# Turning the normalised rows of five pairs by DMA instead of TensorE, and grouping the half-width products, in a one-core attention and feed-forward kernel

## The chip, the core and the metric

The kernel runs on one core of one Trainium2 chip. The metric is the device time of one launch in microseconds; the median of three runs before the change is 612.24 us (612.08 to 613.53).

## The reference

`x` is 16 sequences of 64 rows of 1024; `ctx_4096` is 16 matrices of 1024 x 1024, all float32. Cut to what is computed:

```python
def fake_quant(x, s, z):
    return (clip(round(x / s + z), 0, 255) - z) * s

x = x + matmul(fake_quant(layernorm(x)), fake_quant(ctx_4096))      # one matrix per sequence
h = layernorm(x)
q, k, v = split(h @ qkv_w + qkv_b, 3)                               # 32 heads of 32
q, k = rope(q), rope(k)
p = softmax(q @ k.T / sqrt(32) + causal mask)
x = x + (p @ v) @ out_w + out_b
h = layernorm(x)
x = x + h @ W.T + bias + sum_e coeffs[e] * scales[e] * (h @ A[e].T) @ Bf[e].T
```

## The kernel before, in words

The rows of two sequences form a pair of 128 rows; there are eight pairs, 0 to 7. For each pair the kernel does the quantised cross product with its two context matrices, then attention; the feed-forward stage follows for all pairs. Every large product is made of float16 parts: operands are split into a high and a low float16 part, and `dense` (L1347) makes three products for each of eight slices of 128: high by high, high by low, low by high. A tile is 128 rows by 512 columns in one PSUM bank, 24 products.

The five engines have programs of their own, joined by semaphores, and the order on each is written out by hand. TensorE's order sets the plan: `next_pair(i, ahead)` (L1700) makes the six projection tiles of pair `i` with `qkv(i, j, between)` (L1447), where `between` is a table {slice: [steps]} of what else is issued behind which slice. Among these steps:

- `codes` turns the quantised rows of pair `i + 1` (eight float16 transposes, L1436), and ScalarE evacuates them in `a_high` (L385); `codes_turned` waits for that. `t(...)`, which is `cross` (L1406), multiplies them with the context codes. From pair 3 on ("tiled") one product has half the width of the array (128 by 64) and two run side by side; `shifted`, `cross_shift` (L1422), adds a correction from the sums of all codes. The products come in four groups of eight, behind slices of tiles 2, 2, 3 and 5, and the shift in a fifth group.
- `qk_turn`, `scores`, `p_turn` and `values` are the attention of pair `i`. `project` (L1538) is the output projection in four parts of twelve products. After the second, `x_turn(i + 1)` turns the normalised rows of the next pair: eight float32 transposes (`turn`, L1344) into the PSUM banks T.

The turned rows are evacuated by ScalarE as the high float16 part (`x_high`, L380) and by VectorE as the low one (`x_low`, L933). TensorE starts pair `i + 1` when `s_xl` says that both are there. VectorE makes the rows in `norm2` (L924): statistics, a chain of small operations for the reciprocal root, then `lnt = (x - mean) * factor`. Before that it needs `tiled_evac` (L955), which needs the shift products, which need `sums_as_f16` (L950), which needs GpSimd's sums of all 16 code chunks (`add_codes`, L800).

The context comes in 16 chunks of 512 KB for each pair. SP loads them (`load_chunk`, L650; order in `next_set`, L723) into three slots in turn: the two halves of `raw`, and `lnt`, which is also where the normalised rows lie until they are turned. Chunk `c` uses slot `c % 3`; chunk 2, the first one in `lnt`, waits for the row turn. ScalarE quantises a chunk into one of eight places of a ring `code` (`quantise`, L357); a place is free again when TensorE and GpSimd have used it. ScalarE's order is in `next_pair` (L493): two chunks of pair `i + 2` at the end of pair `i`, then chunks 2 to 5 of the next, `a_high`, and the rest between evacuations and exponentials. ScalarE also issues the load of the rows of pair `i + 2` (`rows_after_next`, L400).

In the last stage rows are turned by DMA already: `rows_high` (L621) writes float16 rows and issues a transposing DMA from ScalarE's queue, VectorE's `rows_low` (L1272) makes the low rows, and `rows_low_turned` (L632) turns them.

Of the kernel before, what the change touches and what calls it, by code (L numbers as in the profile page):

```python
# [55 lines left out]
def build(nc, x, ctx_in, consts, qkv_w, out_w, bias_rows, out_bias, ffn_wt, ffn_bias, lora_a, lora_b, lora_w, out):  # L56
# [6 lines left out]
    with es:  # L63
# [51 lines left out]
        uses = [len(range(n, CHUNKS, 3)) for n in range(3)]  # L115
# [10 lines left out]
        d16 = pr[:, 0, :].bitcast(F16)  # L126
        acc_words = acc[:, :].bitcast(I32).rearrange("p (b n) -> p b n", b=2)
# [62 lines left out]
        s_xl = sem("s_xl")  # L190
        s_u8 = sem("s_u8")
# [144 lines left out]
        def _(act):  # L336
# [20 lines left out]
            def quantise(i, c):  # L357
# [3 lines left out]
                else:  # L361
                    n = c % 3
                    src = slots[n].rearrange("p (a n) -> p a n", a=2)
                    if isinstance(i, int) and i == 1:
                        src = chunk1_stage(c)
                        act.wait_ge(s_ctx0[c], 32)
                    else:
                        act.wait_ge(s_slot[n], 16 * (uses[n] * (i - 2) + c // 3 + 1))
# [124 lines left out]
            def next_pair(i, more, late=False):  # L493
# [7 lines left out]
                w(25)  # L501
                q(2)
                if not late:
                    q(3, 4, 5)
                a_high(i + 1, 0)
                a_high(i + 1, 1)
                if late:
                    q(3, 4)
# [3 lines left out]
                qk_evac(i, 0)  # L512
                if not late:
                    q(6)
                q(7, 8)
                w(28)
                qk_evac(i, 1)
                q(9)
                w(29)
                q(10)  # L520
                if late:
                    q(11)
                exponent(i, 0)
                if not isinstance(i, int) or i < PAIRS - 2:
                    rows_after_next(i)
                q(12 if late else 11)
                exponent(i, 1)
                qk_evac(i, 2)
                if not late:
                    q(12)  # L530
                q(13)
                p_evac(i, 0)
                if late:
# [7 lines left out]
                else:  # L541
                    q(14)
# [14 lines left out]
                x_high(i + 1, 0)  # L557
                x_high(i + 1, 1)
                if late:
                    value_bias()  # L560

# [47 lines left out]
            with act.Fori(2, PAIRS - 2) as i:  # L609
# [39 lines left out]
        def _(sp):  # L649
            def load_chunk(i, c):  # L650
# [7 lines left out]
                n = c % 3  # L658
# [1225 lines left out]
```

## Time and profile before

| | |
|---|---|
| Median of 3 runs | 612.24 us |
| The profiled execution's own time | 612.36 us |
| Its span | 610.3 us |
| Granted clock, mean | 1.0 of full |
| TensorE products (PE) busy | 588.4 us, 96% |
| VectorE (DVE) busy | 467.0 us, 77% |
| ScalarE (ACT) busy | 292.8 us, 48% |
| GpSimd (POOL) busy | 125.4 us, 21% |
| Chain that ended last, by engine | PE 79%, DVE 11%, SPq 4%, DMA 3% |

PE, DVE, ACT and POOL are TensorE, VectorE, ScalarE and GpSimd; PEld is TensorE's weight load, SP issues DMAs. A row of a timeline gives start, length, engine, line, operation, output <- input, shapes and count; in brackets stands how long the engine was idle before it, and who ended that. Product durations overlap in the pipeline, so the distance of two starts is what a product costs in a stream. "DMA to landing" is the time from the issue of a transfer to its completion.

### The profile page before, as it was taken

To read this page: it belongs to the slowest core of one execution; us is meant where nothing else is said; L and a number is where in the kernel's file an instruction comes from. 1 tells how busy PE (TensorE), PEld (TensorE's weight loads), DVE (VectorE), ACT (ScalarE), POOL (GpSimd) and SP (SyncE) were. 2 spreads that over 40 slices of the span, in tenths; PEclk is the share of its full clock that TensorE was granted. 3 is DMA by queue.
4 is the path that set the end of the run, shared out by engine and by line. 5 is a ranking of instruction groups with operands and counts; after the bars stand their busy time and mean duration, and the time that the engine had idled before them with its cause. 6 is when DMAs were issued, how large, how long until landed. Compare 5 with 4: busy or idle time off the path is not lost.

```text
span 610.3 us, 12961 instructions
## 1 busy us (share of the span) xinstructions
PE 588.4 (96%) x4921; PEld 295.1 (48%) x4921; DVE 467.0 (77%) x931; ACT 292.8 (48%) x359; POOL 125.4 (21%) x173
## 2 busy tenths in 40 slices
PE   3889999999999999999999999999999999999998
PEld 1464455455545445544455445545445554444445
DVE  6999998778777866786677868678864789987751
ACT  5977695865456435634553464546331242210100
POOL 4000010000165234613541354345100000000000
PEclk9999999999999999999999999999999999999999
DMA  8999996861356255507531673265222025477541
GB/s 319 387 387 361 393 361 227 287 225 71 132 188 233 71 201 205 180 35 275 203 141 50 224 237 107 114 208 194 103 92 81 1 89 223 122 147 154 144 107 53
DMA packets 53698, 111.83 MB, mean 183 GB/s; under 512 B 18586, under 2 KB 18970, under 8 KB 53664
## 3 DMA queue, kind: packets, MB, share of 16 engines
q1 hardware_dynamic: 37744, 104.35, 49.4%
q10 hardware_dynamic: 15648, 6.48, 4.6%
q0 software_dynamic: 272, 0.55, 0.2%
q8 instruction: 21, 0.34, 0.2%
q14 instruction: 13, 0.11, 0.1%
HBM read 99.30 MB, written 8.39 MB: 176 GB/s over the span
## 4 chain that ended last, share of the span: by engine, by line
PE 79%; DVE 11%; SPq 4%; DMA 3%; issue 2%; ACT 1%; ACTq 0%; DVEq 0%
PE dense L1353 15%; PE dense L1355 15%; PE dense L1354 15%; PE turn L1344 5%; PE dense L1547 4%; PE dense L1549 4%; PE dense L1548 4%; DVE wq L941 4%; PE cross L1417 3%; PE score L1508 3%; PE dense L1563 2%; SPq L656 2%; DMA wq<-in_qkv_w 2%; PE cross L1402 2%; PE score L1534 2%
## 5 line engine op out<-in xcount | busy, mean ns | idle before, releaser
L1353 PE MATMUL dense<-wq,xn_h 128*128 128x512 f16 x400 | 152.2, 380 | 1.3 <-DMA xn_l<-spare 0.9
L1354 PE MATMUL dense<-wq,xn_h 128*128 128x512 f16 x400 | 151.6, 379 | 0.0
L1355 PE MATMUL dense<-wq,xn_l 128*128 128x512 f16 x400 | 151.6, 379 | 0.0
L811 POOL TENSOR_TENSOR acc<-code,acc 128x256 int32<-128x256 int32 x140 | 104.0, 773 | 114.1 <-ACT code L378 114.1
L378 ACT ACTIVATE code<-raw,cst,qc 128x1024 uint8<-128x1024 f32 x72 | 87.3, 1237 | 13.4 <-DMA raw<-in_ctx 12.9
L1353 PEld LDWEIGHTS dense<-wq,xn_h 128*128 128x128 f16 x400 | 39.0, 97 | 50.6 <-issue 14.0
L1355 PEld LDWEIGHTS dense<-wq,xn_l 128*128 128x128 f16 x400 | 39.1, 98 | 47.3
L1354 PEld LDWEIGHTS dense<-wq,xn_h 128*128 128x128 f16 x400 | 39.2, 98 | 34.9
L378 ACT ACTIVATE code<-lnt,cst,qc 128x1024 uint8<-128x1024 f32 x32 | 39.6, 1237 | 27.0 <-DMA lnt<-in_ctx 26.5
L998 DVE SCALAR_TENSOR_TENSOR at<-cst,score 128x512 f32<-128x512 f16 x24 | 16.4, 684 | 40.1 <-PE score L1508 40.1
L1547 PE MATMUL dense<-wo,rope 128*128 128x512 f16 x112 | 42.5, 379 | 0.8 <-DVE rope L1028 0.8
L1549 PE MATMUL dense<-wo,rope 128*128 128x512 f16 x112 | 42.4, 379 | 0.0
L1548 PE MATMUL dense<-wo,rope 128*128 128x512 f16 x112 | 42.4, 379 | 0.0
L407 ACT ACTIVATE at<-at 128x512 f32<-128x512 f32 x32 | 20.0, 628 | 37.5 <-DVE at L1004 37.4
L394 ACT ACTIVATE at<-turn 128x512 f32<-128x512 f32 x32 | 19.0, 593 | 37.2 <-PE turn L1344 24.0
L811 POOL TENSOR_TENSOR acc<-code,lw 128x256 int32<-128x256 int32 x20 | 11.6, 613 | 116.4 <-ACT code L378 116.4
L413 ACT ACTIVATE at<-turn 128x512 f32<-128x512 f32 x32 | 19.0, 592 | 32.3 <-PE turn L1344 32.2
L626 ACT ACTIVATE spare<-lnt 128x1024 f16<-128x1024 f32 x7 | 7.4, 1057 | 54.1 <-DVE lnt L1259 54.1
L1402 PE MATMUL cross<-code,q1t 128*128 128x512 f16 x96 | 28.3, 392 | 3.2 <-DVE xa L948 1.5
L984 DVE TENSOR_TENSOR rope<-dense,cst 128x512 f32<-128x512 f32 x32 | 22.0, 689 | 11.2 <-PE dense L1355 8.3
L990 DVE TENSOR_TENSOR rope<-rope 128x512 f32<-128x512 f32 x32 | 24.5, 766 | 1.4
L1035 DVE SCALAR_TENSOR_TENSOR xa<-dense,xa 128x512 f32<-128x512 f32 x16 | 11.0, 690 | 18.1 <-PE dense L1549 18.0
(225 smaller groups left out, 1036.3 us busy)
## 6 DMA issues: line engine op xcount, KB each, us to landing
raw<-in_ctx SPq DMA_DIRECT2D x72, 512.0 KB, 4.4
lnt<-in_ctx SPq DMA_DIRECT2D x32, 512.0 KB, 4.2
wo<-in_ctx SPq DMA_DIRECT2D x16, 512.0 KB, 8.8
wo<-in_qkv_w SPq DMA_DIRECT2D x12, 512.0 KB, 11.7
wq<-in_qkv_w SPq DMA_DIRECT2D x8, 512.0 KB, 11.9
x_scratch<-xa SPq DMA_DIRECT2D x8, 512.0 KB, 3.0
wq<-in_ctx SPq DMA_DIRECT2D x7, 512.0 KB, 11.7
wo<-in_out_w SPq DMA_DIRECT2D x7, 512.0 KB, 6.9
```

Of the source, the lines that this page charges most:

```text
L378: act.activation(low_bytes, src, ACT.Identity, scale=qc[:, 1:2], bias=z2).then_inc(s_u8, 1)
L811: ins = pool.tensor_tensor(sums[:, cols], words[:, cols], acc_from.to_broadcast([P, half]) if c < 2 else sums[:, cols], ALU.add)
L941: dve.scalar_tensor_tensor(lo, staged(j), WSC, hi, ALU.mult, ALU.subtract).then_inc(s_wlo, 1)
L990: dve.tensor_tensor(rope[:, 2 + j % 2, :], rope[:, 0, :], rope[:, 1, :], ALU.add).then_inc(s_qr, 1)
L1344: ins = pe.transpose(bank[:, k * P:(k + 1) * P], src[:, c:c + P], ident)
L1353: pe.matmul(bank[:, :], a_h[:, k, :], w_hi, start=(k == 0 and not started), stop=False)
L1354: pe.matmul(bank[:, :], a_h[:, k, :], w_lo, start=False, stop=False)
L1355: ins = pe.matmul(bank[:, :], a_l[:, k, :], w_hi, start=False, stop=(k == KC - 1 and not last))
L1402: ins = pe.matmul(X[n][:, :], lhs, code[:, c % RING, n * NT:(n + 1) * NT], start=(kc == 0), stop=(kc == KC - 1))
L1547: pe.matmul(D[n][:, :], c_h[:, k, :], wo_h[:, k, cols], start=(k == 0), stop=False)
L1548: pe.matmul(D[n][:, :], c_h[:, k, :], wo_l[:, k, cols], start=False, stop=False)
L1549: ins = pe.matmul(D[n][:, :], c_l[:, k, :], wo_h[:, k, cols], start=False, stop=(k == KC - 1))
```

## The change

1. **Rows by DMA.** For pairs 3 to 7 `x_turn`, `x_high` and `x_low` go. ScalarE computes the high float16 rows straight from `xb` with factor and bias (`rows_turned`) and turns them by a transposing DMA into `xn_h`; VectorE writes the low rows (`x_rows_low`), and ScalarE issues their turn into `xn_l`. The float16 rows lie in `pr`, the tile of the softmax. The first projection tile of such a pair makes its sixteen products with the high rows first, and then waits for the low ones.
2. **Chunks.** The first six chunks alternate between the halves of `raw`; `lnt` is used by chunks 6, 9, 12 and 15. SP loads six chunks of pair `i + 2` ahead, but holds the fifth (and what follows) until the low turn of the pair before has landed. ScalarE quantises four chunks of pair `i + 2` at the end of pair `i`.
3. **Products.** Code products come in two groups of sixteen: behind the last slice of tile 2, and behind slice 1 of tile 5, there with the shift.
4. VectorE casts the code sums before `softmax_in(i, 3)`. The loops of ScalarE and SP over pairs 2 to 5 are written out.

```diff
+        slot_of = [c % 2 if c < 6 else (c - 4) % 3 for c in range(CHUNKS)]
+        x_hl = [pr[:, n, :].bitcast(F16) for n in range(2)]
...
+            def rows_turned(i):
+
+                act.wait_ge(s_xfac, i - TILED + 1)
+                act.activation(x_hl[0], xb[:, :], ACT.Identity, scale=nw[:, 0:1], bias=nw[:, 3:4]).then_inc(s_xrowh, 1)
+                act.wait_ge(s_xrowh, i - TILED + 1)
+                act.wait_ge(s_qkv, 6 * i)
+                act.dma_start_transpose(xn_h[:, :, :], x_hl[0]).then_inc(s_xturnh, 16)
+                act.wait_ge(s_xt, 2 * i + 2)
+                act.dma_start_transpose(xn_l[:, :, :], x_hl[1]).then_inc(s_xturnl, 16)
...
+                    q(4, 5, 6, 7)
+                    a_high(i + 1, 0)
+                    a_high(i + 1, 1)
+                    qk_evac(i, 0)
+                    qk_evac(i, 1)
+                    q(8)
+                    exponent(i, 0)
+                    if not isinstance(i, int) or i < PAIRS - 2:
+                        rows_after_next(i)
+                    q(9, 10)
+                    exponent(i, 1)
+                    q(11)
+                    qk_evac(i, 2)
+                    q(12)
+                    p_evac(i, 0)
+                    q(13)
                     qk_evac(i, 3)
-                    q(15)
+                    q(14, 15)
                     p_evac(i, 1)
                 exponent(i, 2)
+                if more:
+                    quantise(i + 2, 0)
                 exponent(i, 3)
+                if more:
+                    quantise(i + 2, 1)
...
                 if more:
-                    quantise(i + 2, 0)
-                    quantise(i + 2, 1)
+                    quantise(i + 2, 2)
+                    quantise(i + 2, 3)
                 c_high(i, 1)
...
+                else:
+                    rows_turned(i + 1)
...
-                if c == 2:
+                if c < 2:
+                    sp.wait_ge(s_u8, CHUNKS * i + c - (1 if isinstance(i, int) and i == 2 else 2))
+                elif c < 6:
+                    sp.wait_ge(s_u8, CHUNKS * i + c - 1)
+                    if c == 4 and tiled(i):
+                        sp.wait_ge(s_xturnl, 16 * (i - 2))
+                elif c == 6:
                     sp.wait_ge(s_xt, 2 * i)
...
+            def x_rows_low(i):
+                dve.wait_ge(s_xn, i + 1)
+                dve.wait_ge(s_xrowh, i - TILED + 1)
+                dve.tensor_tensor(x_hl[1], lnt[:, :], x_hl[0], ALU.subtract).then_inc(s_xt, 2)
...
+                    for k in range(KC):
+                        for w in (wq_h, wq_l):
+                            pe.matmul(D[0][:, :], xn_h[:, k, :], w[:, k, n * NT:(n + 1) * NT], start=(k == 0 and w is wq_h), stop=False)
+                    pe.wait_ge(s_xturnl, 16 * (i - 1))
+                    for k in range(KC):
+                        pe.matmul(D[0][:, :], xn_l[:, k, :], wq_h[:, k, n * NT:(n + 1) * NT], start=False, stop=False)
...
-                    qkv(i, 2, {1: [at(t, 0, 1)], 3: [at(codes_turned, 1), at(qk_turn, i, 1)], 4: [at(m, 1)], 6: [at(middle_biases, i), at(scores, i, 0)], 7: [at(t, 2, 3)]})
+                    qkv(i, 2, {4: [at(codes_turned, 1), at(qk_turn, i, 1), at(m, 1)], 6: [at(middle_biases, i), at(scores, i, 0)], 7: [at(t, 0, 1, 2, 3)]})
...
-                    qkv(i, 3, {2: [at(m, 2)], 5: [at(t, 4, 5)], 6: [at(turned, i, 1), at(qk_turn, i, 2)]})
+                    qkv(i, 3, {2: [at(m, 2)], 6: [at(turned, i, 1), at(qk_turn, i, 2)]})
...
-                    qkv(i, 5, {0: [at(t, 6, 7)], 1: [at(m, 4)], 2: [at(m, 5)], 3: [at(values_due, i, 0)], 4: [at(values, i, 0)],
-                               6: [at(shifted), at(evacuated, i, 0), at(p_turn, i, 2)], 7: [at(p_turn, i, 3)]})
+                    qkv(i, 5, {1: [at(t, 4, 5, 6, 7), at(shifted), at(m, 4)], 2: [at(m, 5)], 3: [at(values_due, i, 0)], 4: [at(values, i, 0)],
+                               6: [at(evacuated, i, 0), at(p_turn, i, 2)], 7: [at(p_turn, i, 3)]})
...
-                if ahead:
+                if late:
                     x_turn(i + 1)
```

## Rows read from the trace of the kernel before

**Rows 1.** the page: busy us and its share; granted clock in 40 slices
```profile
PE 588.4 (96%) x4921; PEld 295.1 (48%) x4921; DVE 467.0 (77%) x931; ACT 292.8 (48%) x359; POOL 125.4 (21%) x173
...
PEclk9999999999999999999999999999999999999999
```

**Rows 2.** windows: one pair, busy us of each engine, clock, DMA
```profile
332.00:389.00 57.00, 56.77 (x541) 28.18 (x539) 42.53 (x88) 29.26 (x36) 22.98 (x32) 1.00 0.49 166
```

**Rows 3.** the chain of waits: start us, us, what, at the row turns
```profile
331.36 0.87 PE turn L1344 x8
...
388.60 0.87 PE turn L1344 x8
```

**Rows 4.** the timeline of TensorE in pair 5: tile starts
```profile
337.25 0.38 PE L1353 MATMUL dense<-wq,xn_h 128*128 128x512 f16 x1
...
347.84 0.60 PE L1344 MATMUL turn<-cst,rope 128*128 128x128 f32 x4
```

**Rows 5.** the timeline of TensorE around the row turn
```profile
330.98 0.38 PE L1549 MATMUL dense<-wo,rope 128*128 128x512 f16 x1
331.20 1.04 PE L1344 MATMUL turn<-cst,lnt 128*128 128x128 f32 x8
332.07 0.38 PE L1547 MATMUL dense<-wo,rope 128*128 128x512 f16 x1
```

**Rows 6.** row turns of L1344: duration ns min/median/max, first and last start
```profile
L1344 PE MATMUL turn<-cst,lnt x72: 272/273/328, 37.1 to 512.7; 128*128 128x128 f32 x72
```

**Rows 7.** the timeline of TensorE around one group of half-width products
```profile
350.00 0.38 PE L1355 MATMUL dense<-wq,xn_l 128*128 128x512 f16 x1
350.31 1.05 PE L1417 MATMUL cross<-code,q1t 128*64 128x512 f16 x8
351.30 0.39 PE L1353 MATMUL dense<-wq,xn_h 128*128 128x512 f16 x1
```

**Rows 8.** VectorE's timeline from the second scores to the pair's end
```profile
371.64 0.69 DVE L998 SCALAR_TENSOR_TENSOR at<-cst,score 128x512 f32<-128x512 f16 x1 [2.16 <-PE score L1508]
...
381.48 0.75 DVE L1028 SCALAR_TENSOR_TENSOR rope<-score,rope 128x256 f16<-128x256 f32 x2
...
382.74 0.68 DVE L846 BATCH_NORM_STATS2 st<-xb 128x6 f32<-128x512 f32 x1
...
386.53 0.81 DVE L931 TENSOR_SCALAR lnt<-xb,mv,nw 128x1024 f32<-128x1024 f32 x1
```

**Rows 9.** the timeline of TensorE at the start of the output projection
```profile
382.37 0.38 PE L1547 MATMUL dense<-wo,rope 128*128 128x512 f16 x1 [0.16 <-DVE rope L1028]
```

**Rows 10.** the timeline of the last stage, a row turn by DMA
```profile
544.68 1.06 ACT L626 ACTIVATE spare<-lnt 128x1024 f16<-128x1024 f32 x1 [7.39 <-DVE lnt L1259]
...
545.76 1.31 ACTq L630 DMA_TRANSPOSE q1t<-spare  x1
545.77 1.23 DVE L1276 TENSOR_TENSOR spare<-lnt,spare 128x1024 f16<-128x1024 f32 x1 [0.52 <-ACT spare L626]
```

**Rows 11.** the instructions on xn_l: its transposing DMAs
```profile
DMA to landing us min/median/max: 3.7/6.1/7.0
```

**Rows 12.** DMA issues: count, median us to landing; the turns into q1t
```profile
q1t<-spare ACTq DMA_TRANSPOSE x8, 3.5
```

**Rows 13.** the timeline of ScalarE at a pair's start
```profile
335.91 1.24 ACT L378 ACTIVATE code<-lnt,cst,qc 128x1024 uint8<-128x1024 f32 x1 [2.99 <-DMA lnt<-in_ctx]
338.44 2.44 ACT L378 ACTIVATE code<-raw,cst,qc 128x1024 uint8<-128x1024 f32 x2 [1.28 <-DMA raw<-in_ctx]
...
345.87 1.08 ACT L387 ACTIVATE q1t<-turn 128x512 f16<-128x512 f32 x2 [0.54 <-PE turn L1436]
```

**Rows 14.** instructions of L679, SP's chunk loads from 325 to 400
```profile
DMA to landing us min/median/max: 3.1/4.7/7.3
```

**Rows 15.** the timeline of GpSimd, sums of the last four chunks
```profile
366.38 6.43 POOL L811 TENSOR_TENSOR acc<-code,acc 128x256 int32<-128x256 int32 x8 [4.08 <-ACT code L378]
```

**Rows 16.** the instructions of L403, loads of a later pair's rows
```profile
DMA to landing us min/median/max: 4.0/6.8/7.3
```

More of the change, by code:

```diff
@@ L114, in build @@
         slots = [raw[:, 0, :], raw[:, 1, :], lnt[:, :]]
-        uses = [len(range(n, CHUNKS, 3)) for n in range(3)]
+        slot_of = [c % 2 if c < 6 else (c - 4) % 3 for c in range(CHUNKS)]
+        uses = [slot_of.count(n) for n in range(3)]
         value_stage = [at_stage[:, 1, :, :], at_stage[:, 0, :, :], at_stage[:, 2, :, :], spare[:, :].rearrange("p (a n) -> p a n", a=2)] + o_stage[0:4]
@@ L190, in build @@
         s_xl = sem("s_xl")
+        s_xfac = sem("s_xfac")
+        s_xrowh = sem("s_xrowh")
+        s_xturnh = sem("s_xturnh")
+        s_xturnl = sem("s_xturnl")
         s_u8 = sem("s_u8")
@@ L500, in w @@
                         weight_hi(j)
[L501 to L506, printed above, removed]
                 if late:
+                    w(25)
+                    q(2)
+                    a_high(i + 1, 0)
+                    a_high(i + 1, 1)
                     q(3, 4)
@@ L511, in next_pair @@
                     w(27)
[L512 to L524, printed above, removed]
+                    qk_evac(i, 0)
+                    q(7, 8)
+                    w(28)
+                    qk_evac(i, 1)
+                    q(9)
+                    w(29)
+                    q(10, 11)
+                    exponent(i, 0)
                     rows_after_next(i)
[L526 to L529, printed above, removed]
                     q(12)
-                q(13)
-                p_evac(i, 0)
-                if late:
+                    exponent(i, 1)
+                    qk_evac(i, 2)
+                    q(13)
+                    p_evac(i, 0)
                     p_evac(i, 1)
@@ L608, in _ @@
             next_pair(1, True, True)
-            with act.Fori(2, PAIRS - 2) as i:
+            for i in range(2, PAIRS - 2):
                 next_pair(i, True)
@@ L657, in load_chunk @@
                     return
-                n = c % 3
+                n = slot_of[c]
                 if isinstance(i, int) and i == 1:
@@ L1126, in next_pair @@
                 softmax_in(i, 2)
+                if not late:
+                    sums_as_f16(i + 1)
                 softmax_in(i, 3)
@@ L1144, in next_pair @@
                 c_low(i, 1)
-                x_low(i + 1, 0)
-                x_low(i + 1, 1)
+                if late:
+                    x_low(i + 1, 0)
+                    x_low(i + 1, 1)
+                else:
+                    x_rows_low(i + 1)
                 out_evac(i, 0)
@@ L1726, in codes_turned @@
                         pe.wait_ge(s_ah, 2 * i + 3 + e)
-                pe.wait_ge(s_xl, 2 * i + 2)
+                if isinstance(i, int) and i == 1:
+                    pe.wait_ge(s_xl, 2 * i + 2)
+                else:
+                    pe.wait_ge(s_pte, 4 * i)
+                    pe.wait_ge(s_xturnh, 16 * (i - 1))
                 if isinstance(i, int) and i == 1:
```

49 lines of the change are left out of this document (31 added, 18 removed).

## The prediction

> **What bounds the kernel now.** First the page's busy shares: TensorE is busy for 588.4 of 610.3 us and its granted clock stands at the upper level, 2.4 GHz, in every slice [rows 1]. Then the windows by pair: one steady pair has 56.77 us of TensorE in 57.00, with VectorE at 42.53 and ScalarE at 29.26 [rows 2]. The chain of waits shows the same point of two successive pairs 57.24 us apart [rows 3]. TensorE's own stream sets the time, so a product taken out of it is time taken out, as long as the engines that feed it still arrive. Those margins are small, and the change moves nearly all of them. So the work has two halves: what leaves the stream, and what is late next. Offsets below count from the first product of a pair's projections, 337.25 in the pair that I read [rows 4].
>
> **Part 1, turning the rows.** Eight float32 transposes start at 331.20 between two products of the output projection, and the next product starts at 332.07: 0.87 us [rows 5]. They go for pairs 3 to 7 (the fourth to the eighth): 5 x 0.87 = 4.35 us. A transpose's own duration is 273 ns [rows 6], but the durations overlap. The Trainium skill, "TensorE: Matmul & The Clock Gate", section "Part 4: PE-mode transpose", gives about 275 ns for one in a kernel; 40 at that price would be an estimated 11 us. The starts decide here, and they say 0.109 us each.
>
> **Part 2, grouping.** A product of 512 columns takes 0.216 us in the stream (330.98 to the next start, 331.20) [rows 5]. Around a group of eight half-width products the starts are 350.00, 350.31 and 351.30 [rows 7]: 1.30 from the full product before to the one after, less its own 0.216, is 1.08, of which the eight, running two at a time, need 4 x 0.216 = 0.86. The other 0.22 is entering and leaving. The shift products have the same form. A pair has five such groups now and two afterwards: 3 x 0.22 = 0.66, in the five pairs 2 to 6 that prepare the next one, 3.3 us. Bounds: nothing, if the larger groups pay inside, and 3.3. I take 3.3, since it is a difference of starts.
>
> **Part 3, VectorE between the second scores and the output projection.** VectorE starts that softmax at 371.64 and ends the first low half of the attention result at 381.48 + 0.75 = 382.23 [rows 8], 10.6 us in one piece. The same instructions stand there afterwards, only that the cast of the code sums comes two steps earlier. TensorE waits for its end by 0.16 [rows 9], once in each of five pairs. The later group puts 0.66 more of TensorE's own work into that stretch (chunks 8 to 15 and the shift in one group, 0.86 x 3 + 0.22 = 2.8, where 2 x 1.08 stood), so the wait is filled: 0.8 us, bounds 0 and 0.8, I take 0.8.
>
> **Part 4, the new path of the rows, and its cover.** By my count TensorE reaches the output projection at offset 43.9 and the next pair at 55.15 (48 products of 0.216 and the value products, 11.25, and no turn). VectorE starts the statistics at 44.4 at the latest, after the last value tile, and has the factor 3.8 us later (382.74 to 386.53) [rows 8]. With one more small operation (0.2) that is 48.4. ScalarE writes the high rows from there; the like step of the last stage takes 1.06 [rows 10]: 49.5. It issues the high transpose (1.31) [rows 10] and then needs the low rows, which VectorE has at 51.2 (48.4, 0.81 for the normalised rows, 0.75 for the low half [rows 8], 1.23 for the subtraction [rows 10]). The low transpose is issued there. In the last stage such transposes landed after 3.7, 6.1 and 7.0 us into one pair of tiles [rows 11] and after 3.5 in the median into the other [rows 12], the slow ones beside stores and row loads. Afterwards nothing of size is in flight, since chunk 4 is held back: I take 3.5 to 3.7, high at 53.1, low at 54.8. TensorE wants high at 55.15, and low only after sixteen products, 55.15 + 16 x 0.216 = 58.6. Even at 7.0 low lands at 58.2. So this wait costs 0; for the high one at 7.0 the bound is 1.4 x 5 = 7. The Trainium skill, "DMA: Bandwidth & Descriptors", section "Anatomy of one DMA", has 2.0 us plus the bytes at 436 GB/s, for a copy issued from GpSimd: an estimated 2.6 us for these 256 KB. The traces' 3.5 is longer, and by either the cost is 0. VectorE's and ScalarE's own work for the step stays about the same and falls into their idle time: 0.
>
> **Part 5, the chunk loads behind the transposes.** SP issues chunks 4 and on from offset 54.9, which is -0.25 of the next pair. At present the turn is over by 332.07 [rows 5], and the first chunk that it lets go is taken by ScalarE at 335.91, the second at 338.44, the third right behind [rows 13]: 3.8 and 6.4 us later. So chunk 4 is there at 3.6, 5 at 6.1, 6 with 7.3. Chunk 7, issued when ScalarE is done with chunk 4 (4.8), comes 3.1 to 4.7 us later (least and median of such loads [rows 14]), 7.9 to 9.5. Each takes ScalarE 1.24 [rows 13]: all four are done at 9.8 to 10.7. Behind them in its queue stands the evacuation of the turned codes, 1.08 for two halves [rows 13], the first at 10.3 to 11.3. TensorE asks for it at offset 10.59, where it now turns the first query tile (347.84) [rows 4]. So no wait, or 0.7 us, in pairs 3 to 6 (four times; pair 2's loads follow a row turn that stays as it was). I take 0.25 each, +1.0; bounds 0 and +2.8. Nobody else needs the codes before TensorE: their products come eight microseconds later.
>
> **Part 6, ScalarE in the middle of the pair.** The first eight chunks' products now run at 18.8 to 20.7, so chunk 8's place in the ring is free at 19.4. Then eight chunks of 1.24, three evacuations and two exponentials of about 0.6 must pass ScalarE. I get chunk 11 at 26.3, the third query/key evacuation at 26.9 (TensorE asks at 27.6), the last chunk at 33.6, GpSimd's sums, 1.6 a chunk when back to back (6.43 for four) [rows 15], at 35.3, the cast at 36.1, and the shift asks at 37.2. All in time, with 0.7 to 1 us to spare. But chunk 11's load is issued with that of the row pair, and chunk loads take up to 7.3 us [rows 14], the row loads 4.0 to 7.3, median 6.8 [rows 16]. A slow one brings chunk 11 at 28.0 in place of 25.0, the evacuation behind it at 29.9, and TensorE waits 2.3. Four pairs have it; I charge one, +2.3, bounds 0 and +9.2.
>
> Edits with one answer: the unrolled loops of ScalarE and SP, the early loads of chunks 2 to 5 and the quantising of four chunks instead of two at the pair's end lie in idle time of engines at half load: 0. If that cover were gone, two more chunks, 2.5 us, would push the high rows past their 2.0 of room (53.1 against 55.15), 0.5 a pair.
>
> **Sum.** -4.35 - 3.3 - 0.8 + 1.0 + 2.3 = -5.15 against the profiled execution's 612.36 (span 610.3): 607.2. Its time is 0.12 above the median of the runs, 612.24, which I count as equal.
>
> **Rivals.**
> (a) ScalarE late in most pairs with row loads (Part 6 in two or three, Part 5 at its bound). For it: row loads with a median of 6.8, and one queue that quantises, evacuates and issues. Against: some landed in 4.0. Time: 612.36 - 8.45 + 2 or 3 x 2.3 + 0 to 2.8, 609 to 613.
> (b) Slower: the hold on chunk 4 puts the first four chunks, and with them the codes' evacuation, behind TensorE's need. Place: the wait on the codes in the second tile of pairs 3 to 6. If the low transpose takes 7.0 in place of 3.6 and chunk 7 lands after 4.7, the codes come at 11.3 + 3.4 = 14.7, 4.1 beyond the need; 4 x 4.1 = 16.4, time 612.36 - 8.45 + 16.4 = 620.3. It decides from a wait of 8.45 / 4 = 2.1 us in each of the four pairs. Against it: only these transposes should be in flight. The Trainium skill's DMA page, section "Rules for kernel authors", says that a transpose next to ordinary DMAs needs nothing; by that the hold would be needless, and its price stays.
> (c) TensorE gives back more than the starts show, nearer 273 ns a transpose: 612.36 - 11 - 3.3 + 1 = 599. Against: back-to-back starts.
> (d) Nothing comes of it: VectorE's 10.6 us piece and the statistics set the pair, and TensorE waits elsewhere: about 612.
>
> **How the numbers follow.** Forecast 607.2 (own range 603 to 609.5): 0.60. (a) 0.18, (b) 0.13, (c) 0.04, (d) 0.05. 0.3%, about what a measurement of this kernel can tell from no change, is 1.8 us, so faster is below 610.4. Faster: 0.60 + 0.04 + nearly half of (a), 0.08 = 0.72. Same: the rest of (a), 0.10, and (d) = 0.15. Slower: 0.13. With every wait at 0 the time is 603.9; the range starts at 602.5, for small waits that I have not counted, and ends at 615, which takes in (a), (d) and the mild part of (b). It leaves out some 0.14.
>
> **What would show it.** Right: the same point of two pairs about 55.5 us apart, no transposing DMA among TensorE's releasers in pairs 3 to 7, low transposes landing within 4 us, TensorE's wait on the code evacuation near 0.3 a pair, and one wait near 2 us on a ScalarE evacuation. Wrong: waits of over 2 us a pair on the codes' evacuation, with ScalarE in turn waiting for its chunk loads (b), or a period still near 57.2 with VectorE named before TensorE's idle time (d). Part 2 is wrong if sixteen half-width products take more than 1.95 us between full ones.

## The result and the profile after

The changed kernel takes 617.94 us (median of 5 runs, 616.28 to 618.86) where the kernel before takes 612.67 (5 runs beside it, 612.08 to 613.63). The ratio is 1.0083, with a 95% interval of 1.0065 to 1.0101: slower by 5.3 us, where 5.15 us less was forecast. The profiled execution is the one of 617.94, its span is 616.1.

The page after, busy times and granted clock, answering to [rows 1]:

```profile
PE 585.4 (95%) x4881; PEld 293.0 (48%) x4881; DVE 476.9 (77%) x931; ACT 293.5 (48%) x354; POOL 138.8 (23%) x173
...
PEclk9999999979999999999999999999999999999999
```

TensorE is busy 3.0 us less and the span is 5.8 us longer. One of the 40 slices, the ninth (123 to 139 us), has a lower clock, 0.7. The next rows are waits, summed (engine, line, what it waited for: us in total, times, longest). L1389 is a turn, L1600 the output projection, L937 `out_base`, L994 the cast of the code sums, L384 `quantise`:

```profile
ACT code L384 <- DMA raw<-in_ctx: 47.5, 14, 8.1
...
DVE xa L937 <- DMA x_scratch<-xa: 6.4, 3, 5.3
...
PE turn L1389 <- DVE rope L1031: 3.6, 2, 3.3
...
PE dense L1600 <- DVE rope L1069: 3.1, 6, 0.6
DVE acc L994 <- POOL acc L842: 3.1, 5, 0.6
...
PE turn L1389 <- ACT q1t L403: 2.8, 4, 1.0
```

Of these waits of TensorE the kernel before shows the one for L1069's counterpart, and that only 0.16 us long, in each of five pairs [rows 9]. Now it waits for VectorE before the output projection up to 0.6 us, for the evacuated codes up to 1.0, and once 3.3 us for VectorE behind a store. The profile counts a wait from the modelled end of the product before; by starts, less the 0.216 us of that product, such a wait is 0.15 longer. The sums below say which of the two they use. No wait of TensorE for a transposing DMA of pairs 3 to 7 is there.

**Where the 5.8 us are.** The starts of the first score products (`scores(i, 0)`, 64 small products) mark the pairs. Before they are at 71.9, 125.4 and 183.7 us, then 57.24 apart like the row turns [rows 3], and the eighth pair's at 470.9; after at 71.7, 131.6 and 189.2, then 57.75, 57.20, 57.33 and 57.29 apart, the last at 476.9. The second pair's, before and then after:

```profile
125.41 1.16 PE L1508 MATMUL score<-at 32*64 32x64 f32 x64
```

```profile
131.59 1.16 PE L1561 MATMUL score<-at 32*64 32x64 f32 x64
```

So the first pair-to-pair distance grew from 53.5 to 59.9 us, 6.4 us and so a little more than the whole loss, and everything after it came out nearly even: the steady pairs, which should have saved 1.53 us each, saved nothing. These are two questions.

**The second pair.** The chain of waits there (start us, us, what):

```profile
108.64 3.43 DMA raw<-in_ctx
112.09 1.25 ACT code L384
113.73 7.10 DMA x_scratch<-xa
120.86 1.24 DVE xa L937
...
124.29 0.70 DVE rope L1031
```

The chain runs through a load of a chunk into `raw` and its quantising, and then a DMA `x_scratch<-xa`: the store of the first pair's rows, issued at 113.73 and landed 7.1 us later. VectorE's `out_base` waits for it, because it overwrites `xa`, and the wait is 5.3 us (the row of L937 above). The timeline of SP before and after shows what moved (start us, us of issuing, line, output <- input, count); L702 and L733 are the store, L679 and L710 chunk loads:

```profile
104.25 0.91 SPq L679 DMA_DIRECT2D raw<-in_ctx  x2
107.13 0.35 SPq L702 DMA_DIRECT2D x_scratch<-xa  x1
108.83 0.33 SPq L679 DMA_DIRECT2D lnt<-in_ctx  x1
```

```profile
108.64 3.48 SPq L710 DMA_DIRECT2D raw<-in_ctx  x2
...
113.36 0.33 SPq L710 DMA_DIRECT2D raw<-in_ctx  x1
113.73 0.43 SPq L733 DMA_DIRECT2D x_scratch<-xa  x1
```

Before, the store goes out at 107.13, behind three loads that were free to go. After, it stands behind chunks 2 to 7 of the third pair. Of these chunk 5 needs ScalarE to have quantised chunk 3, and chunk 7 needs chunk 4, and ScalarE comes to these two chunks only at 110.53 and 112.09, between splits of weights and the evacuation of the codes. The store goes out 6.6 us later, with chunk loads around it. TensorE at that place (timeline, then windows with us, busy us of PE, PEld, DVE, ACT and POOL, granted clock, DMA share and GB/s):

```profile
121.45 0.38 PE L1400 MATMUL dense<-wq,xn_l 128*128 128x512 f16 x1
125.13 1.08 PE L1389 MATMUL turn<-cst,rope 128*128 128x128 f32 x4 [3.30 <-DVE rope L1031]
126.01 0.63 PE L1398 MATMUL dense<-wq,xn_h 128*128 128x512 f16 x1
126.44 0.63 PE L1399 MATMUL dense<-wq,xn_h 128*128 128x512 f16 x1
```

```profile
121.50:125.00 3.50, 0.33 (x2) 0.00 (x0) 3.40 (x7) 2.04 (x3) 0.00 (x0) 0.90 0.32 124
125.00:128.00 3.00, 2.87 (x9) 1.58 (x10) 1.79 (x2) 2.59 (x4) 0.00 (x0) 0.50 0.79 214
128.00:131.00 3.00, 3.00 (x9) 0.84 (x7) 0.55 (x1) 3.00 (x4) 0.00 (x0) 0.50 0.69 212
```

By starts it waits from 121.67 to 125.13 (3.46 us). After that wait the granted clock is 0.50, the level of 1.2 GHz, from 125 to 131, and the starts lie 0.43 apart in place of 0.216: half of those 6 us, some 2.9, is lost. Together that is the 6.4 us of this distance.

**The steady pairs.** First the wait for the codes, in the pair whose projections start at 343.29 (the counterpart of [rows 4]). TensorE asks 10.59 us after that first product, as before:

```profile
353.66 0.38 PE L1400 MATMUL dense<-wq,xn_l 128*128 128x512 f16 x1
354.91 0.54 PE L1389 MATMUL turn<-cst,rope 128*128 128x128 f32 x3 [0.88 <-ACT q1t L403]
```

ScalarE's quantising and the first evacuation of the codes:

```profile
345.78 1.24 ACT L384 ACTIVATE code<-raw,cst,qc 128x1024 uint8<-128x1024 f32 x1 [7.85 <-DMA raw<-in_ctx]
...
353.06 1.24 ACT L384 ACTIVATE code<-raw,cst,qc 128x1024 uint8<-128x1024 f32 x1 [2.73 <-DMA raw<-in_ctx]
354.21 1.06 ACT L403 ACTIVATE q1t<-turn 128x512 f16<-128x512 f32 x2
```

SP's loads and its store:

```profile
342.54 0.80 SPq L710 DMA_DIRECT2D raw<-in_ctx  x2
...
347.05 0.33 SPq L710 DMA_DIRECT2D raw<-in_ctx  x1
347.42 0.43 SPq L733 DMA_DIRECT2D x_scratch<-xa  x1
```

ScalarE sat idle 7.85 us for chunk 4, which SP held, and quantised chunks 4, 5 and 6 without a long wait. Chunk 7 was issued at 347.05, the store at 347.42, and chunk 7 reached ScalarE at 353.06, 6.0 us after its issue, so the codes were evacuated at 354.21 and TensorE, ready at 353.88, started at 354.91. The waits of the four pairs are 0.60, 0.35, 0.88 and 0.95 as the profile counts them, 2.8 us, and 3.4 by starts.

The second scores and the output projection of the same pair, answering to [rows 8] and [rows 9], VectorE and then TensorE; L1039 is the mask, L994 the cast, L1069 the low half of the attention result, L1462 the sixteen code products, L1474 the shift:

```profile
377.45 0.69 DVE L1039 SCALAR_TENSOR_TENSOR at<-cst,score 128x512 f32<-128x512 f16 x1 [2.44 <-PE score L1561]
...
380.28 0.69 DVE L994 CAST acc<-acc 128x2048 f16<-128x2048 uint16 x1 [0.62 <-POOL acc L842]
...
388.01 0.74 DVE L1069 SCALAR_TENSOR_TENSOR rope<-score,rope 128x256 f16<-128x256 f32 x2
```

```profile
379.83 1.92 PE L1462 MATMUL cross<-code,q1t 128*64 128x512 f16 x16
381.58 1.03 PE L1474 MATMUL cross<-acc,lw 128*64 128x512 f16 x8
...
388.90 0.38 PE L1600 MATMUL dense<-wo,rope 128*128 128x512 f16 x1 [0.53 <-DVE rope L1069]
```

VectorE's piece from the second scores to the low half took 10.6 us before (371.64 to 382.23) and now runs from 377.45 to 388.75, 11.3 us. The cast waits 0.62 for GpSimd, in every pair (3.1 us over five). So the low half is late and TensorE waits 0.53. The sixteen code products themselves do what was counted: 1.75 us from their first to the shift's first.

By starts these waits account for the steady pairs. The four distances from 189.2 to 418.7 sum to 229.6 us; 4 x (57.24 - 1.53) is 222.8. Between them lie the codes' waits, 3.4, and 1.8 more than before at the output projection. Three single waits for VectorE add 1.5 (0.73, 0.43 and 0.33). That is 6.7 of 6.7: what the change takes out of TensorE's stream did go, and waits of the same size took its place.

The row turns: L397 turns the high rows, L399 the low ones (duration ns min/median/max, first and last start, then us to landing):

```profile
L397 ACTq DMA_TRANSPOSE xn_h<-at x5: 1257/1263/1323, 223.6 to 452.0; - x5
...
DMA to landing us min/median/max: 3.1/3.3/3.3
```

```profile
L399 ACTq DMA_TRANSPOSE xn_l<-at x5: 1283/1297/1356, 225.0 to 453.4; - x5
...
DMA to landing us min/median/max: 3.2/3.2/5.2
```

Both are quick, as assumed in the forecast; one low turn of the five took 5.2 us, and TensorE did not wait for it.

### The profile page after: what moved, and what is told of

It is laid out like the page before. It is cut to its first block, busy times and chain, and to the rows that moved or that the text cites. A ratio compares the mean times of both kernels' runs of the same rounds, so it can differ in the third digit from the quotient of the medians.

```text
span 616.1 us, 12528 instructions
## 1 busy us (share of the span) xinstructions
PE 585.4 (95%) x4881; PEld 293.0 (48%) x4881; DVE 476.9 (77%) x931; ACT 293.5 (48%) x354; POOL 138.8 (23%) x173
## 4 chain that ended last, share of the span: by engine, by line
PE 43%; DVE 25%; DMA 14%; issue 6%; ACT 5%; SPq 4%; POOL 1%; ACTq 1%; DVEq 0%; POOLq 0%
PE dense L1398 8%; PE dense L1400 8%; PE dense L1399 8%; DMA raw<-in_ctx 5%; ACT code L384 4%; DVE wq L982 4%; PE turn L1389 3%; DMA lnt<-in_ctx 3%; SPq L683 2%; DMA wq<-in_qkv_w 2%; PE dense L1616 2%; PE score L1561 2%; PE dense L1600 2%; PE cross L1447 2%; PE dense L1602 2%
## 5 line engine op out<-in xcount | busy, mean ns | idle before, releaser
L842 POOL TENSOR_TENSOR acc<-code,acc 128x256 int32<-128x256 int32 x140 | 114.6, 845 | 143.5 <-ACT code L384 143.0
L1398 PE MATMUL dense<-wq,xn_h 128*128 128x512 f16 x352 | 134.6, 382 | 1.2 <-DMA xn_l<-spare 0.6
L1399 PE MATMUL dense<-wq,xn_h 128*128 128x512 f16 x352 | 134.2, 381 | 0.0
L1400 PE MATMUL dense<-wq,xn_l 128*128 128x512 f16 x352 | 134.2, 381 | 0.0
L384 ACT ACTIVATE code<-raw,cst,qc 128x1024 uint8<-128x1024 f32 x78 | 95.6, 1236 | 65.3 <-DMA raw<-in_ctx 47.5
L1400 PEld LDWEIGHTS dense<-wq,xn_l 128*128 128x128 f16 x352 | 34.6, 98 | 42.1 <-issue 0.8
L1398 PEld LDWEIGHTS dense<-wq,xn_h 128*128 128x128 f16 x352 | 34.5, 98 | 42.0 <-issue 10.0
L1399 PEld LDWEIGHTS dense<-wq,xn_h 128*128 128x128 f16 x352 | 34.6, 98 | 30.9 <-issue 0.6
L1600 PE MATMUL dense<-wo,rope 128*128 128x512 f16 x112 | 42.5, 380 | 3.4 <-DVE rope L1069 3.1
L1039 DVE SCALAR_TENSOR_TENSOR at<-cst,score 128x512 f32<-128x512 f16 x24 | 16.4, 684 | 35.3 <-PE score L1561 35.3
L384 ACT ACTIVATE code<-lnt,cst,qc 128x1024 uint8<-128x1024 f32 x26 | 32.2, 1237 | 5.8 <-DMA lnt<-in_ctx 5.4
L842 POOL TENSOR_TENSOR acc<-code,lw 128x256 int32<-128x256 int32 x20 | 14.5, 747 | 81.6 <-ACT code L384 72.5
L1389 PE MATMUL turn<-cst,rope 128*128 128x128 f32 x128 | 20.1, 280 | 6.5 <-DVE rope L1031 3.6
```

What stands on the lines that cost most here:

```text
L384: act.activation(low_bytes, src, ACT.Identity, scale=qc[:, 1:2], bias=z2).then_inc(s_u8, 1)
L842: ins = pool.tensor_tensor(sums[:, cols], words[:, cols], acc_from.to_broadcast([P, half]) if c < 2 else sums[:, cols], ALU.add)
L1389: ins = pe.transpose(bank[:, k * P:(k + 1) * P], src[:, c:c + P], ident)
L1398: pe.matmul(bank[:, :], a_h[:, k, :], w_hi, start=(k == 0 and not started), stop=False)
L1399: pe.matmul(bank[:, :], a_h[:, k, :], w_lo, start=False, stop=False)
L1400: ins = pe.matmul(bank[:, :], a_l[:, k, :], w_hi, start=False, stop=(k == KC - 1 and not last))
```

## The experiments

All times below are medians, beside runs of the kernel before on the same chip in the same job; the ratio is to those, with its 95% interval. The kernel before had 612.49 us in the job of e1 to e4, 612.64 in that of e5 to e8, 612.27 in that of e9 and e10, 612.40 in that of e11 and e12. A difference between runs of two jobs (e5 against e1, e9 and e10 against e6, any run against the changed kernel's 617.94) is uncertain by such a few tenths.

**e1: the store between chunks 6 and 7.**

```diff
-                for c in range(6, 8):
-                    load_chunk(i + 1, c)
-                store_x2(i - 1)
-                for c in range(8, CHUNKS):
+                load_chunk(i + 1, 6)
+                store_x2(i - 1)
+                for c in range(7, CHUNKS):
                     load_chunk(i + 1, c)
```

> The changed kernel with one edit: SP issues the store of the pair before (store_x2) between chunks 6 and 7, not behind chunk 7. Theory A (order): the second pair lost 6.2 us because the store of the first pair's rows stood behind chunk 7 of the next, whose slot comes free late there, and the vector engine's out_base waited for it; with the store in front 617.9 - 6.2 = 611.7. Theory B (crowding): the store is slow (7.1 us) because the six early chunk loads crowd it, whatever the order; then 616 to 618 stays.

Measured 611.75 us, ratio 0.9996 (0.9983 to 1.0008). That is the 6.2 us less of theory A, but not for its reason. The store of the second pair hardly moved, since chunk 6 in front of it also leaves late:

```profile
113.62 0.43 SPq L733 DMA_DIRECT2D x_scratch<-xa  x1
```

```profile
DVE xa L936 <- DMA x_scratch<-xa: 4.3, 1, 4.3
```

It goes out at 113.62 where the change has 113.73; only chunk 7 now follows it. VectorE waits 4.3 us for it in place of 5.3 and TensorE 2.4 in place of 3.3, and the clock stayed at its upper level in this profile. So the second pair still takes 57.0 us between first scores, not 53.5: 2.9 less than in the change, which is about what the fall of the clock cost there. The four steady pairs became 0.85 shorter each (57.39 to 56.55 in the mean), with waits for the codes of 1.6 in place of 2.8. Of the 7.4 us between the two profiles 2.9 lie in the second pair and 3.4 in the steady ones; the agreement with theory A is chance.

The mean granted clock of each of the twelve runs prices the fall. Nine runs have 0.999 or 1.0 and a median of 611.69 us; three have 0.997, and take 613.07, 613.51 and 614.31: 1.8 us more. In e4 the like difference is 1.9 us (five runs and two). All five runs of the changed kernel have 0.994 or 0.997.

**e2: the kernel before, its store behind chunk 7.**

```diff
-                for c in range(2, 5):
+                for c in range(2, 8):
                     load_chunk(i + 1, c)
                 store_x2(i - 1)
-                for c in range(5, CHUNKS):
+                for c in range(8, CHUNKS):
```

> The kernel before with one edit: the store of the pair before stands behind chunk 7 in SP's order and not behind chunk 4. Theory A (order): the same loss appears without anything else of the change, 612.4 + 5 to 6.5 = 617 to 619. Theory B (crowding by early loads): no early loads here, so 612 to 613.

Measured 615.93 us, ratio 1.0057 (1.0043 to 1.0070). The late store alone, with nothing else of the change, costs 3.4 us: theory A's mechanism, at about 60% of its size. The rows of that place are SP's, and the sums of VectorE's waits for the store and of TensorE's for VectorE:

```profile
113.16 0.43 SPq L702 DMA_DIRECT2D x_scratch<-xa  x1
```

```profile
DVE xa L904 <- DMA x_scratch<-xa: 6.2, 2, 4.7
...
PE turn L1344 <- DVE rope L990: 3.0, 2, 2.2
```

```profile
126.00:128.00 2.00, 2.00 (x6) 0.68 (x5) 1.23 (x1) 2.00 (x4) 0.00 (x0) 0.50 0.83 260
```

The store goes out at 113.16, and 4.7 us of waiting follow, where the change has 5.3. The first distance is 57.6 in place of 53.5, and the second 59.3 in place of 58.3. This profile is of the slowest of the six runs, 617.90, and the only one whose mean clock is below 1.0: of its first distance 2.4 us are TensorE's wait by starts and 1.7 the clock, which is at half from about 125.0 to 128.4. The two waits alone, 2.4 and 1.0 by starts, make the 3.4 of the median.

**e3: no hold of chunk 4**, on e1.

```diff
                     sp.wait_ge(s_u8, CHUNKS * i + c - 1)
-                    if c == 4 and tiled(i):
-                        sp.wait_ge(s_xturnl, 16 * (i - 2))
```

> The store in front as in the run before it, and SP's wait of chunk 4 for the low turn taken out, so that chunks 4 and 5 load beside the transposing DMAs. Theory C (the hold makes TensorE wait for the codes, 0.76, 0.51, 1.03 and 1.11 us in four pairs, and the transposes have room): 611.7 - 3.4 = 608.3. Theory D (the transposes land after 6 to 7 us beside loads, later than their room of 2 us for the high one): 0 to 1.4 us a pair come back in five pairs, 608.3 to 615.

Measured 609.11 us, ratio 0.9948 (0.9930 to 0.9967). Theory C, at 2.6 of its 3.4 us. The low turns do become slower beside the loads:

```profile
DMA to landing us min/median/max: 4.9/5.1/5.5
```

5.1 us in the median and 5.5 at most, where the change has 3.2, and high turns still 3.1 to 3.3. TensorE asks for the low part so late that it never waits. So the change pays for quiet that the turns don't need. The Trainium skill, "DMA: Bandwidth & Descriptors", section "Rules for kernel authors", says that a transpose next to ordinary DMAs needs nothing. It says so beside the rule that keeps transposes of different queues apart for the data's sake, and gives no time; the price beside loads is this run's, 1.9 us on the low turn's landing and nothing in TensorE's stream.

**e4: the codes before chunk 7**, on e1.

```diff
-                    q(4, 5, 6, 7)
+                    q(4, 5, 6)
                     a_high(i + 1, 0)
                     a_high(i + 1, 1)
+                    q(7)
```

> The store in front, the hold kept, and the scalar engine evacuates the turned codes before it quantises chunk 7. If TensorE's wait for the codes is what chunk 7's late landing costs (3.4 us in four pairs) and nothing behind it is later for it: 611.7 - 3.4 = 608.3. If the pair is set by the vector engine's chain before the output projection (waits of 0.53 to 0.62 there now), the gain moves into that wait and 610.5 to 611.7 stays.

Measured 609.66 us, ratio 0.9955 (0.9940 to 0.9971). That is 2.1 us less than e1, and no wait for the codes is left among TensorE's. Its profile has the clock at half in the second pair, from about 124.2 to 127.6, after a wait of 2.4 us as long as e1's, where it did not fall.

**e5: the first store further in front**, on e1.

```diff
-            for c in range(6):
+            for c in range(4):
                 load_chunk(2, c)
+            store_x2(0)
+            for c in range(4, 6):
+                load_chunk(2, c)
...
                 load_chunk(i + 1, 6)
-                store_x2(i - 1)
+                if i > 1:
+                    store_x2(i - 1)
```

> The store in front as in e1_store_first, and in the second pair further in front still: before chunks 4 and 5 of the third pair, which wait for quantising. In e1 that pair still took 56.95 us between first scores where the kernel before takes 53.48, with one wait of 2.4 us of TensorE behind the vector engine's wait of 4.3 us for the store. Theory A (order of SP alone): these 3.5 us go, 608.3. Theory B (the store is crowded by chunk loads in the air whatever its place): at most 1 us goes, 610.5 to 611.7.

Measured 609.08 us, ratio 0.9946 (0.9930 to 0.9962). The store goes out at 106.57 and the first distance between scores is 53.48 us, exactly that of the kernel before. No wait of VectorE for the store is left. This is theory A, and the clean test of it: here the store really goes out early. The whole is 0.8 above what it gave; the codes' waits sum to 3.7 in this profile where e1's had 1.6.

```profile
106.57 0.33 SPq L733 DMA_DIRECT2D x_scratch<-xa  x1
```

**e6: e5 without the hold and with the codes first.**

```diff
-                    if c == 4 and tiled(i):
-                        sp.wait_ge(s_xturnl, 16 * (i - 2))
...
-                    q(4, 5, 6, 7)
+                    q(4, 5, 6)
                     a_high(i + 1, 0)
                     a_high(i + 1, 1)
+                    q(7)
```

> All three edits on the changed kernel: store in front, no hold of chunk 4, codes evacuated before chunk 7. If the two waits are one and the same (the codes), e3 and e4 do not add: 608.3 - 2.6 = 605.7. If they add: 603.6. If the transposes get late beside loads once the rest is faster: 607 to 608.5.

Measured 605.70 us, ratio 0.9888 (0.9874 to 0.9903). The two edits together give 3.4 on e5, where they gave 2.6 and 2.1 alone on e1, so they partly remove the same wait. The profile is of the slowest of the four runs, 607.26. This is 12.2 us below the changed kernel and 6.9 below the one before.

**e7: the rows turned by TensorE**, groups and orders as in e5, without the hold. `x_turn`, `x_high` and `x_low` are back for all pairs.

```diff
-                if late:
-                    x_turn(i + 1)
+                if ahead:
+                    x_turn(i + 1)
...
-                    rows_turned(i + 1)
+                x_high(i + 1, 0)
+                x_high(i + 1, 1)
...
-                    x_rows_low(i + 1)
+                x_low(i + 1, 0)
+                x_low(i + 1, 1)
```

> Store in front as in e5, groups of sixteen and the new order of chunks, but the rows of all pairs turned by TensorE as before (no transposing DMA, so no hold). Theory: TensorE's stream gets 4.35 us back against e5, but without the hold the codes' wait (1.6 to 3.4 us in all) is gone: 608.3 + 4.35 - 2.6 = 610.0. Rival: the transposes on DMA are what costs and the groups alone are worth their full 3.3 and more: 606 to 608.5.

Measured 610.01 us, ratio 0.9952 (0.9938 to 0.9965), as the theory had it. e6 is 4.3 us faster in the same job, the 4.35 that five turns of 0.87 take in TensorE's stream [rows 5]. e6 also has the codes in front of chunk 7, but neither profile has a wait for the codes, so that order should not count.

**e8: five groups where they stood before**, on e5, with ScalarE's new order.

```diff
-qkv(i, 2, {4: [at(codes_turned, 1), at(qk_turn, i, 1), at(m, 1)], 6: [...], 7: [at(t, 0, 1, 2, 3)]})
+qkv(i, 2, {1: [at(t, 0, 1)], 3: [at(codes_turned, 1), at(qk_turn, i, 1)], 4: [at(m, 1)], 6: [...], 7: [at(t, 2, 3)]})
-qkv(i, 3, {2: [at(m, 2)], 6: [...]})
+qkv(i, 3, {2: [at(m, 2)], 5: [at(t, 4, 5)], 6: [...]})
-qkv(i, 5, {1: [at(t, 4, 5, 6, 7), at(shifted), at(m, 4)], ...})
+qkv(i, 5, {0: [at(t, 6, 7)], 1: [at(shifted), at(m, 4)], ...})
```

> Store in front as in e5, rows by DMA with the hold, but code products in the four groups of eight and the shift alone in the fifth, as before. Theory: 3 x 0.22 x 5 = 3.3 us come back to TensorE's stream, while the wait of 0.6 us a pair for GpSimd's last sum (the vector engine's cast) goes, since ring places come free sooner: 608.3 + 3.3 - 2 = 609.6. Rival: the larger groups save nothing inside, then 606 to 608.3.

Measured 631.54 us, ratio 1.0309 (1.0293 to 1.0326). Both theories missed: my edit was no test of the grouping. The groups stand again in the middle of tiles 2 and 3, but ScalarE quantises chunk 8 and on only after its exponentials and evacuations, so TensorE waits for chunks. The two orders belong together. TensorE's waits on the first code product of a group, summed:

```profile
PE cross L1465 <- ACT code L384: 11.7, 5, 2.4
```

They are half of the 22.5 us that e8 takes more than e5. The groups' own 3.3 and the clock have a share in the rest: all five runs have a mean granted clock of 0.992 to 0.997.

**e9: five groups near the places of the two**, on e6 (in place of e8).

```diff
-qkv(i, 2, {..., 7: [at(t, 0, 1, 2, 3)]})
+qkv(i, 2, {..., 7: [at(t, 0, 1)]})
-qkv(i, 3, {2: [at(m, 2)], ...})
+qkv(i, 3, {0: [at(t, 2, 3)], 2: [at(m, 2)], ...})
-qkv(i, 5, {1: [at(t, 4, 5, 6, 7), at(shifted), at(m, 4)], 2: [at(m, 5)], ...})
+qkv(i, 5, {0: [at(t, 4, 5)], 1: [at(t, 6, 7), at(m, 4)], 2: [at(shifted), at(m, 5)], ...})
```

> e6 with the same code products at nearly the same places, but in five groups (8, 8, 8, 8 and the shift) with one slice of full products between them. It mends e8, where the groups stood before the scalar engine had their chunks. If entering and leaving costs 0.22 us a group: 3 x 0.22 x 5 = 3.3 more, 609.0; less up to 1.3 where the wait for values (0.74 a pair) fills up. If the grouping saves nothing: 605.7.

Measured 607.41 us, ratio 0.9918 (0.9905 to 0.9932), 1.7 us above e6, which ran in another job; by the two ratios it is 1.8. Grouping does save, but about half of the 3.3 us. Some of the rest is given back as waiting: TensorE's waits before the output projection sum to 2.8 in e6 and to 2.1 here.

**e10: shift and cast back in their old places**, on e6. The shift goes behind slice 6 of tile 5, the cast behind `softmax_out(i, 2)`; three groups in all.

```diff
-                    qkv(i, 5, {1: [at(t, 4, 5, 6, 7), at(shifted), at(m, 4)],
+                    qkv(i, 5, {1: [at(t, 4, 5, 6, 7), at(m, 4)],
-                               6: [at(evacuated, i, 0), at(p_turn, i, 2)],
+                               6: [at(shifted), at(evacuated, i, 0), at(p_turn, i, 2)],
...
-                if not late:
-                    sums_as_f16(i + 1)
                 softmax_in(i, 3)
...
                     softmax_out(i, 2)
+                    sums_as_f16(i + 1)
                     softmax_out(i, 3)
```

> e6 with the shift products back behind slice 6 of tile 5 and the vector engine's cast back behind softmax_out(i, 2), as in the kernel before; the four groups of chunks stay two. If the waits of TensorE for the vector engine in e6 (0.74, 0.61 and 0.25 a pair, in the kernel before 0.24 and 0.16) come from the early cast and its wait of 0.62 for GpSimd: 605.7 - 5 x (1.2 - 0.22) = 600.8. If the rows of the next pair come later for it and the high turn runs over its room: 605.7 or more.

Measured 605.58 us, ratio 0.9887 (0.9871 to 0.9902). The mechanism is there: VectorE's wait for GpSimd is gone, TensorE's before the projection is 0.8 over five as before, and the four steady pairs are 55.86 or 55.87 us long, which is 57.24 - 0.87 - 2 x 0.22 = 55.93. But the time stays that of e6, not 600.8: I had taken the 0.74 wait for values, read in one pair of e6, for a wait of all. The same pairs of e6 take 56.2 in the mean, so 1.3 in four pairs was all there was.

```profile
PE dense L1601 <- DVE rope L1071: 0.8, 5, 0.2
```

The profiled span is 1.5 shorter, 603.9 against 605.4, but e6's profile is of its slowest run and its three others have spans of 603.8 and 603.9; the medians differ by 0.1 only. By the count, 2.0 less waiting at the projection against 1.1 for the group that is there again, 0.9 should have come. It didn't show, and why is open. In one job with e9, e10 is 1.8 us faster: it has two groups fewer, 2.2 by the count of 0.22.

**e11: only the first store in front**, on the changed kernel.

```diff
-            for c in range(6):
+            for c in range(4):
                 load_chunk(2, c)
+            store_x2(0)
+            for c in range(4, 6):
+                load_chunk(2, c)
...
-                store_x2(i - 1)
+                if i > 1:
+                    store_x2(i - 1)
```

> The changed kernel with one edit: only the store of the first pair goes in front of chunks 4 and 5 of the third; in all other pairs the store stays behind chunk 7. It splits what e1 and e5 won. If all of the loss by the store lies in the second pair: 617.9 - 6.4 (59.86 to 53.48 between first scores) = 611.5 from that pair, and what e5 has below it, 2.4, is the steady pairs' share. If the steady pairs have no share: 609.

Measured 610.34 us, ratio 0.9961 (0.9947 to 0.9975). The place of this one store is worth 7.6 us. The first distance is 54.2 us, 5.6 less, the clock stays up (in all seven runs), and TensorE's wait for VectorE behind the store is gone. The other 2.0 is not in that place; in the profiles, which are 6.8 apart, the later pairs are 1.4 shorter together, with waits for the codes of 2.3 in place of 2.8. Moving the stores of the steady pairs too (e5) adds 1.3, with intervals that overlap.

**e12: the hold again**, on e10.

```diff
                     sp.wait_ge(s_u8, CHUNKS * i + c - 1)
+                    if c == 4 and tiled(i):
+                        sp.wait_ge(s_xturnl, 16 * (i - 2))
```

> e10 with the one edit that SP's hold of chunk 4 until the low turn has landed is put back; the codes are still evacuated before chunk 7. If the hold costs only through chunk 7 in front of the codes, nothing: 605.6. If chunks 4 to 6 are late for the codes too, TensorE waits 0.3 to 0.6 in four pairs: 607 to 608.

Measured 606.04 us, ratio 0.9894 (0.9880 to 0.9908), no wait for the codes in TensorE's rows. 0.5 above e10 with intervals that overlap: with the codes ahead of chunk 7 the hold costs little or nothing.

## Why the prediction was wrong

The direction was wrong and the time outside the range, by a term that the sum did not have.

**The step that failed.** "Edits with one answer: the unrolled loops of ScalarE and SP, the early loads of chunks 2 to 5 ... lie in idle time of engines at half load: 0." The early loads are not only loads. They stand in SP's queue ahead of the store, each with a wait for ScalarE, and VectorE's `out_base` waits for the store. I traced the loads' own waits and not what they were put in front of, and looked only at a steady pair, where ScalarE is early. In the second pair it also splits weights. The runs show 7.6 us for it (e11), with the distance in that place back at 53.48 when all is put right (e5), and 3.4 when the kernel before gets the late store alone (e2). Some 2 to 3 of the 7.6 are TensorE's clock, which fell after the wait; the forecast had no term for that either. With 7.6 off, the changed kernel is at 610.3, inside the range and faster by 0.4% (e11), but still 3.1 above the 607.2 of the forecast. That remainder lies above all in the sizes of Parts 3 and 5.

**Part 1** held: 4.3 us for 4.35 (e6 against e7). The starts were the right measure, not the 273 ns of rival (c).

**Part 2** held as a size in TensorE's stream: pairs of 55.86 us against a count of 55.93 (e10). But 1.7 us of 3.3 reach the time in e9 against e6.

**Part 3** had the wrong sign. I wrote -0.8 for the wait before the projection; it became 3.1 in place of 0.8, so +2.3. I had the cast at 36.1 and GpSimd done at 35.3, without a wait; in the trace GpSimd's last sum is late by 0.62 in each pair, and VectorE's piece grew from 10.6 to 11.3. Moving shift and cast back restores the wait of 0.8, but not the time (e10).

**Part 4** held: high turns landed after 3.1 to 3.3 us, low ones after 3.2 in the median, and TensorE never waited for them. The cover was larger than it had to be (e3).

**Part 5** had the right place and the wrong size: 2.8 us in four pairs for the 1.0 I took, at the bound of 2.8, and 3.4 by starts, past it. I let chunk 7 land 3.1 to 4.7 us after its issue; it took 6.0, with the store issued 0.4 us behind it. Rival (b) named this wait and the right side of the result, but its price, 16.4 us, was that of slow transposes, which did not occur; its mechanism is not what made the kernel slower.

**Part 6** did not happen: the row loads landed after 3.3 to 4.6 us, not 7, and the 2.3 us were not spent. Rival (a), which needed them in two or three pairs, goes with it; by its own terms its upper end is 613.6 and not 613.

In sum, all by starts in the two profiles: -4.35 for the turns and -3.3 for the groups, +6.4 in the second pair (3.46 wait, 2.9 clock), and in the steady pairs +3.4 for the codes, +1.8 at the projection and +1.5 of single waits, and once more 0.4 at the projection of the seventh pair. That gives 5.9 slower; the spans are 5.8 apart and the medians 5.3.

**Left open.** What the 2.0 of the 7.6 are that don't lie in the second pair. How much of the 7.6 is the clock: it took 2.9 us in the profile of the change, and a run with the fall took 1.8 more than one without in e1 and 2.2 in e2, but how long TensorE waited in the runs without a profile is not known. Why it fell after 2.4 us in e4 and e2 and not in e1. Why the shorter waits of e10 don't show in its time.

## What to carry to other kernels

When a load is moved ahead in an in-order queue, list everything it overtakes, and for each who waits for it; a store is in that list, because something wants its buffer back. Do that for the first and the last turn of a loop too, where the engines that clear the queue's waits have other work: a steady pair showed nothing of the store here, and the second pair held 6.4 us. When an edit brings the time that was expected, look whether it moved what it should have moved: e1 brought its 6.2 us with the second pair's store only 0.1 us earlier. And read a wait in several turns before pricing it; one turn of e6 promised 4.9 us that were not there.

## What the runs showed of the hardware

- After 3.46 us without a product, by starts, TensorE's granted clock stood at half for 6 us, with products 0.43 us apart. After a wait of 2.4, as the profile counts it, it stayed up in e1 and fell for 3.4 us in e4; after one of 2.2 it fell in e2. A run with a mean clock of 0.997 took 1.8 us more than one of 1.0 in e1, 1.9 in e4 and 2.2 in e2.
- Entering and leaving a group of half-width products cost 0.22 us in the kernel before [rows 7]; sixteen of them in a row took 1.75 us, 0.219 for two side by side.
- Transposing DMAs of 128 x 1024 float16 from ScalarE's queue landed 3.1 to 3.3 us after issue in quiet, the second of two after 3.2 in the median and 5.2 at most. Beside 512 KB loads only the second slowed, to 5.1 in the median (e3).
- The 512 KB store to DRAM landed after 3.0 us in the median before and after 6.4 in the change, with chunk loads around it.
